# Transposes of the probabilities moved around masks and scores in an attention and expert layer on one core

## The chip, the cores and the metric

The kernel runs on one core of one Trainium2 chip. The metric is the device time in microseconds (us), the median over several executions.

## The reference, cut to what matters

A decoder layer over 32 batches of 128 tokens with 128 features: self-attention with 16 heads of 8 features and a window of 32 keys, then windowed cross-attention over a context (window 16), then a mixture of 8 experts of which each token takes 2. Each part is added to the running x and starts with a layer norm.

```python
x = x + _L0_attn_ref(_layernorm(x), w_qkv, w_out)
x = x + _L0_xattn_ref(_layernorm(x), ctx_1024, Wq, bq, Wk, bk, Wv, bv, Wo, bo, 1)
x = x + _L0_ffn_ref(_layernorm(x), gate_w, w1, w2)
# in both attentions, for each head
attn = einsum('bhqd,bhkd->bhqk', q, k) * scale
attn = softmax(where(allowed, attn, -inf))
out = einsum('bhqk,bhkd->bhqd', attn, v)
```

## The kernel before, in words

Every engine has its own instruction stream, written out by hand, and the streams meet only at semaphores. A batch of 128 tokens is one item. There are 32 items of the self kind and then 32 of the cross kind; one item's tokens lie on the 128 partitions. After both attentions the expert stage runs 71 blocks of 128 sorted rows (lines 985 to 1093).

The attention is a software pipeline. `attend` (line 270) gives every engine one step per item number c. A step works on several items at once: `runs(h, c, lead)` asks whether item c + lead is there, and the code of that lead runs. A loop body (`Fori`) holds four steps. For c from 27 to 32 the last steps of self are interleaved with the first of cross, piece by piece between the `yield`s.

What happens to one item, by lead:

- TensorE, lead 1: masks into p_scores (L401), then the scores added (L408), in two halves of 8 heads. VectorE takes the row maximum of each half (L718) into shift, and TensorE subtracts it with L453. ScalarE takes the exponential of each half out of p_scores into probs (L556).
- TensorE, lead 0: `turn_probs` (L523) transposes the probabilities of one half into p_probsT, four full 128x128 transposes. There is only one bank p_probsT, so the second half can start only when ScalarE has copied the first half out (`copy_probsT`, L550). Then L513 multiplies the transposed probabilities with the values, 32 matmuls of 32 output columns (64 records, as float32 goes in two passes).
- VectorE divides by the sums (L759, L761) and so makes att. In the next step (lead -1) TensorE transposes att (L437), ScalarE copies it (L579), TensorE projects it (L463) and VectorE adds it to x (L677).
- Further ahead, lead 5 or more down to 2: statistics (L739, L747), L661 and L664 on GpSimd, normalisation (L688), transpose xT (L494) and its copy (L597), q and k (L420, L421 for self; L429, L431 for cross), values (L478) and their four copies (L612).
- Self: ScalarE copies q and k out raw (L567), a DMA on SP swaps neighbouring partitions (L339), GpSimd and VectorE rotate (L637, L701, L705). Cross: ScalarE adds the biases (L572, L573). In both kinds GpSimd then spreads k over four head groups (k_heads, L643), which the scores need.
- Cross only, for routing: x after cross-attention is normalised (xn3, L692), transposed (x3T, L487), copied (L601) and multiplied with the gate (L797); VectorE picks two experts and their slots (L864 to L927). ScalarE fills the rows (L834), and GpSimd sends them with two indirect DMAs, L855, right behind k_heads, for tile c - 6.

The order inside a TensorE step before is: masks and scores, q and k, transpose of att, first `turn_probs`, shift, projection, second `turn_probs`, values with x3T and xT, L513. The order inside a ScalarE step before is: raw copy (self) or biases (cross), attT, first copy, first exponential, second copy, second exponential, then xnT, x3T, values, row.

## Time and profile before

| what | value |
|---|---|
| median of 3 runs | 622.54 us |
| lowest, highest | 619.52, 624.52 us |
| time of the profiled execution | 620.3 us |
| its span, first to last instruction | 617.9 us |
| mean granted TensorE clock | 0.925 of 2.4 GHz |
| TensorE matmul busy | 507.6 us (82%) |
| VectorE busy | 386.4 us (63%) |
| ScalarE busy | 335.4 us (54%) |
| GpSimd busy | 311.0 us (50%) |

The shares are means over stages with different limits, so the steps of each stage are to be read by themselves. Self steps run to about 190 us of the span, cross steps to about 430 us, the experts after that. A row of the timeline holds a run of instructions of one line: start, length, engine, line, operation, output and inputs, shape and count, and in brackets how long the engine stood idle before it and for whom. A matmul's start is when it was issued; when its result is there shows at the engine that waits for it.

### The profile page before, as it was taken

How to read it: one execution, taken by the hardware profiler on the slowest of the kernel's cores; microseconds unless marked ns; L12 is line 12 of the kernel's file. 1: busy time of each engine (PE TensorE's matmuls, PEld its weight loads, DVE VectorE, ACT ScalarE, POOL GpSimd, SP SyncE). 2: the span in 40 equal slices, each digit the busy share in tenths (PEclk: the TensorE clock that was granted, in tenths of full speed). 3: DMA queues.
4: the chain of work that ended last, by engine and by line, in shares of the span. 5: the costliest groups of instructions: out<-in, count | busy, mean ns of one | idle time of the engine just before them, and what ended most of it. 6: DMA issues, size and time to landing. Idle time of an engine off the chain costs nothing.

```text
span 617.9 us, 30506 instructions
## 1 busy us (share of the span) xinstructions
PE 507.6 (82%) x11885; PEld 413.1 (67%) x11885; DVE 386.4 (63%) x1314; ACT 335.4 (54%) x981; POOL 311.0 (50%) x417
## 2 busy tenths in 40 slices
PE   1769999999988988879788888886179999999940
PEld 1446777777765665657576666655069999999940
DVE  4537788888864567666666666654526666665626
ACT  1547677777776776666666666653223444333410
POOL 3524445444453446655555555654605555545533
PEclk9979999999999999998989899986559999999985
DMA  7160000000000001100000001000222222222229
GB/s 225 54 275 30 22 27 27 28 25 25 27 22 12 16 13 30 34 29 26 26 26 26 26 27 30 28 30 19 76 49 71 70 66 68 70 65 61 56 94 328
DMA packets 36481, 34.92 MB, mean 57 GB/s; under 512 B 5934, under 2 KB 32688, under 8 KB 36161
## 3 DMA queue, kind: packets, MB, share of 16 engines
q1 hardware_dynamic: 20144, 15.42, 7.9%
q10 hardware_dynamic: 11952, 10.07, 5.8%
q0 software_dynamic: 4320, 8.53, 4.1%
q8 instruction: 45, 0.74, 0.5%
q14 instruction: 20, 0.16, 0.1%
HBM read 18.58 MB, written 11.68 MB: 49 GB/s over the span
## 4 chain that ended last, share of the span: by engine, by line
PE 58%; issue 14%; another core or an unknown queue 13%; DVE 4%; DMA 3%; ACT 3%; SPq 2%; ACTq 1%; POOL 1%; DVEq 0%; POOLq 0%
PE p_scores L1006 9%; PE p_probsT L523 7%; PE p_att_bank L513 6%; PE p_scores L408 5%; PE p_att_bank L1015 5%; PE p_v_bank L1015 5%; PE p_scores L453 3%; PE p_scores L401 2%; PE p_v_bank L478 2%; PE p_att_bank L463 2%; PE p_qk L420 2%; PE p_v_bank L494 2%; DVE x L312 1%; PE p_scores L1021 1%
## 5 line engine op out<-in xcount | busy, mean ns | idle before, releaser
L643 POOL TENSOR_TENSOR k_heads<-qk,consts 128x512 f32<-128x512 f32 x64 | 66.7, 1042 | 121.0 <-ACT qk L573 65.7
L1091 POOL DMA_INDIRECT expert_results<-weighted,result_at x71 | 74.7, 1053 | 77.0 <-DVE weighted L1079 41.4
L718 DVE TENSOR_REDUCE shift<-p_scores 128x8 bf16<-128x512 f32 x128 | 82.4, 686 | 34.1 <-PE p_scores L408 33.9
L550 ACT COPY probsT<-p_probsT 128x512 f32<-128x512 f32 x128 | 75.6, 591 | 26.1 <-PE p_probsT L523 24.5
L513 PE MATMUL p_att_bank<-values,probsT 128*32 128x36 f32 x4096 | 66.6, 205 | 24.9 <-issue 24.9
L1055 ACT ACTIVATE hidden<-p_scores 128x512 f32<-128x512 f32 x71 | 42.4, 598 | 77.2 <-PE p_scores L1006 52.2
L523 PE MATMUL p_probsT<-consts,probs 128*128 128x128 f32 x512 | 83.1, 287 | 0.5 <-ACT probsT L550 0.2
L513 PEld LDWEIGHTS p_att_bank<-values,probsT 128*32 128x32 f32 x4096 | 53.3, 111 | 39.6 <-issue 32.9
L556 ACT ACTIVATE probs<-p_scores 128x512 f32<-128x512 f32 x128 | 77.9, 609 | 0.1
L1006 PE MATMUL p_scores<-gotT,w_now 128*128 128x128 f32 x568 | 77.8, 281 | 0.0
L855 POOL DMA_INDIRECT sent_rows<-row,slot_u x64 | 64.3, 1004 | 15.8 <-issue 15.5
L1006 PEld LDWEIGHTS p_scores<-gotT,w_now 128*128 128x128 f32 x568 | 71.5, 198 | 0.2 <-ACT gotT L1058 0.2
L612 ACT COPY values<-p_v_bank 32x128 f32<-32x128 f32 x256 | 68.3, 267 | 2.2
L408 PE MATMUL p_scores<-k_heads,qk 32*32 32x256 f32 x2048 | 64.9, 405 | 3.5 <-issue 3.5
L523 PEld LDWEIGHTS p_probsT<-consts,probs 128*128 128x128 f32 x512 | 61.8, 148 | 6.5 <-ACT probsT L550 6.3
L677 DVE TENSOR_TENSOR x<-x,p_att_bank 128x128 f32 (+1 forms) x64 | 18.4, 287 | 55.3 <-PE p_att_bank L463 55.3
L1070 DVE COPY w_now<-w 128x512 f32 x71 | 30.5, 430 | 35.8 <-PE p_scores L1006 29.2
L664 POOL TENSOR_TENSOR rstd<-var_eps,minus_half 128x2 f32<-128x2 f32 (+1 forms) x70 | 44.8, 639 | 5.5
L688 DVE TENSOR_SCALAR xn<-x,mean_var,rstd 128x128 f32 (+1 forms) x64 | 42.2, 659 | 6.2 <-POOL rstd L664 6.2
L453 PE MATMUL p_scores<-shift,minus_ident_bf 128*128 128x256 bf16 x256 | 41.8, 283 | 0.6 <-DVE shift L718 0.4
L597 ACT COPY xnT<-p_v_bank 128x128 f32<-128x128 f32 x64 | 17.3, 270 | 44.9 <-remote 37.0
L1015 PE MATMUL p_att_bank<-w_now,hidden 128*128 128x128 f32 x288 | 39.6, 282 | 1.2 <-ACT hidden L1055 1.1
(131 smaller groups left out, 962.6 us busy)
## 6 DMA issues: line engine op xcount, KB each, us to landing
got<-sent_rows ACTq DMA_DIRECT2D x71, 66.0 KB, 1.9
swapped<-raw SPq DMA_DIRECT2D x64, 64.0 KB, 1.9
w<-w_in ACTq DMA_DIRECT2D x2, 2048.0 KB, 11.9
back<-expert_results SPq DMA_DIRECT2D x8, 512.0 KB, 6.8
ctxT<-ctxT_in SPq DMA_DIRECT2D x32, 64.0 KB, 1.9
out<-x SPq DMA_DIRECT2D x8, 256.0 KB, 5.0
x<-x_in SPq DMA_DIRECT2D x4, 448.0 KB, 10.1
expert_results<-weighted,result_at POOLq DMA_INDIRECT x71
```

Source lines behind the costliest of these rows:

```text
L408: mm = nc.tensor.matmul(p_scores[j * BLK:(j + 1) * BLK, r * G:(r + 1) * G, 0:WIN], qk[r * BLK:(r + 1) * BLK, 0, j * BLK:(j + 1) * BLK], k_ ...
L513: mm = nc.tensor.matmul(p_att[j * BLK:(j + 1) * BLK, r * VROW:(r + 1) * VROW], probsT[:, 4 * (r // HALF) + 2 * ks + r % HALF, j * BLK:(j + ...
L523: mm = nc.tensor.transpose(p_probsT[:, i * P:(i + 1) * P], probs[:, half, ks, r * G:(r + 1) * G, :].rearrange("p g k -> p (g k)"), ident)
L550: nc.scalar.copy(probsT[:, 4 * half:4 * half + 4, :], p_probsT[:, :].rearrange("p (m q) -> p m q", q=P)).then_inc(s_pT, 1)
L556: nc.scalar.activation(probs[:, half, :, :, :].rearrange("p s h k -> p h s k"), p_scores[:, half * 8:half * 8 + 8, 0:WIN].rearrange("p h ( ...
L612: a = nc.scalar.copy(values[lo:lo + BLK, slot, 1:, :, g, 0:HD], p_v[lo:lo + BLK, :].rearrange("p (b r d) -> p b r d", b=NBLK, d=HD))
L643: nc.gpsimd.tensor_tensor(k_heads[:, :, BLK:], qk[:, 1:2, :].to_broadcast([P, G, P]), cv(C_HEAD, G).unsqueeze(2).to_broadcast([P, G, P]), ...
L718: nc.vector.tensor_reduce(shift[:, half * 8:half * 8 + 8], p_scores[:, half * 8:half * 8 + 8, 0:WIN], AX.X, ALU.max).then_inc(s_max, 1)
L855: nc.gpsimd.indirect_dma_start(out=sent, out_offset=bass.IndirectOffsetOnAxis(ap=slot_u[:, t, k:k + 1], axis=0), in_=row[:, t, k, :], in_o ...
L1006: mm = nc.tensor.matmul(p_hidden[half][:, f * P:(f + 1) * P], w1_now[:, half, f * P:(f + 1) * P], gotT[:, half, :], start=True, stop=True)
L1015: mm = nc.tensor.matmul(p_y[half], hidden[:, half, f * P:(f + 1) * P], w2_now[:, half, f * P:(f + 1) * P], start=(f == 0), stop=(f == FC - 1))
L1091: nc.gpsimd.indirect_dma_start(out=results, out_offset=bass.IndirectOffsetOnAxis(ap=result_at[:, slot:slot + 1], axis=0), in_=weighted[:, ...
```

## The change

The first `turn_probs` of an item moves to the front of the TensorE step, ahead of masks and scores; it now waits for the first exponential of its item, which the masks' wait covered before. The second moves right behind the scores. On ScalarE both copies of p_probsT stand first in the step and both exponentials one behind the other; the raw copy of the self kind moves behind the exponentials, and in the cross kind the bias passes stand behind the second copy. GpSimd, VectorE and SP have the same order as before.

```diff
@@ pe_step @@
+                if runs(h, c, 0):
+
+                    n = count(0)
+                    nc.tensor.wait_ge(s_probs, 2 * n + 1)
+                    wait(nc.tensor, s_pT, 2 * n)
+                    turn_probs(0).then_inc(s_pTraw, 1)
+                yield
                 if runs(h, c, 1):
...
                         mm.then_inc(s_scores, 1)
                 yield
+                if runs(h, c, 0):
+
+                    n = count(0)
+                    if not runs(h, c, 1):
+                        nc.tensor.wait_ge(s_probs, 2 * n + 2)
+                    nc.tensor.wait_ge(s_pT, 2 * n + 1)
+                    turn_probs(1).then_inc(s_pTraw, 1)
+                yield
                 if own and runs(h, c, 3):
...
-                if runs(h, c, 0):
-
-                    n = count(0)
-                    if not runs(h, c, 1):
-                        nc.tensor.wait_ge(s_probs, 2 * n + 2)
-                    wait(nc.tensor, s_pT, 2 * n)
-                    turn_probs(0).then_inc(s_pTraw, 1)
-                yield
                 if runs(h, c, 1):
...
-                yield
-                if runs(h, c, 0):
-
-                    n = count(0)
-                    nc.tensor.wait_ge(s_pT, 2 * n + 1)
-                    turn_probs(1).then_inc(s_pTraw, 1)
                 yield
@@ act_step @@
+                if runs(h, c, 0):
+                    copy_probsT(0)
+                yield
+                if runs(h, c, 0):
+                    copy_probsT(1)
+                yield
+                if not own and runs(h, c, 2):
+
+                    n = count(2)
+                    nc.scalar.wait_ge(s_qkraw, n + 1)
+                    nc.scalar.activation(qk[:, 1, :], p_qk[:, P:2 * P], ACT.Identity, bias=cols[:, 1:2])
+                    nc.scalar.activation(qk[:, 0, :], p_qk[:, 0:P], ACT.Identity, bias=cols[:, 0:1]).then_inc(s_qk, 1)
+                yield
+                if runs(h, c, -1):
...
+                yield
+                if runs(h, c, 1):
+                    exponent(0)
+                yield
+                if runs(h, c, 1):
+                    exponent(1)
+                yield
                 if own and runs(h, c, 3):
...
                     nc.scalar.copy(raw[:, (c + 3) % 2, :, :].rearrange("p t k -> p (t k)"), p_qk[:, 0:2 * P]).then_inc(s_raw, 1)
-                if not own and runs(h, c, 2):
...
-                yield
-                if runs(h, c, -1):
...
-                yield
-                if runs(h, c, 0):
-
-                    copy_probsT(0)
-                yield
-                if runs(h, c, 1):
-                    exponent(0)
-                yield
-                if runs(h, c, 0):
-                    copy_probsT(1)
-                yield
-                if runs(h, c, 1):
-                    exponent(1)
-                yield
                 if runs(h, c, 3 + ahead):
```

The changed kernel has a few lines more, so its line numbers run on: masks L408, scores L415, q and k L435, L436 (self) and L444, L446 (cross), att's transpose L452, shift L460, projection L470, values L479, L514 for the probabilities times values, L524 for their transposes, and on ScalarE copies L551, exponentials L557.

TensorE at the start of the first step of the cross loop, before (p_probsT is the bank of the transposed probabilities, p_qk holds q and k):

```order
L401 MATMUL p_scores<-masks_bf,ident_bf 32x4x64 x15
L408 MATMUL p_scores<-k_heads,qk 32x4x64 x16
L425 REGISTER_ALU
L429 MATMUL p_qk<-xnT,wcross 128x128 [waits xT_made]
L430 ISA
L431 MATMUL p_qk<-ctxT,wcross 128x128 [waits ctx_loaded0]
L436 REGISTER_ALU
L437 MATMUL p_att_bank<-consts,att 128x128 [waits att_made]
L294 REGISTER_ALU
L523 MATMUL p_probsT<-consts,probs 128x128 [waits probsT_made]
L523 MATMUL p_probsT<-consts,probs 128x128 x3
```

The same place in the changed kernel:

```order
L524 MATMUL p_probsT<-consts,probs 128x128 [waits probsT_made,probs_made]
L524 MATMUL p_probsT<-consts,probs 128x128 x3
L294 ISA
L404 REGISTER_ALU [waits probs_made]
L408 MATMUL p_scores<-masks_bf,ident_bf 32x4x64 [waits qk_spread]
L408 MATMUL p_scores<-masks_bf,ident_bf 32x4x64 x15
L415 MATMUL p_scores<-k_heads,qk 32x4x64 x16
L524 MATMUL p_probsT<-consts,probs 128x128 [waits probsT_made]
L524 MATMUL p_probsT<-consts,probs 128x128 x3
L440 REGISTER_ALU
L444 MATMUL p_qk<-xnT,wcross 128x128 [waits xT_made]
```

One set of four transposes now stands ahead of the masks and one between the scores and q, k.

ScalarE at the same place, before:

```order
L572 ACTIVATE qk<-p_qk,cols 128x128 [waits qk_in_psum]
L573 ACTIVATE qk<-p_qk,cols 128x128
L578 REGISTER_ALU
L579 COPY attT<-p_att_bank 128x128 [waits attT_in_psum]
L549 ISA
L550 COPY probsT<-p_probsT 128x512 [waits probsT_in_psum]
L555 ISA
L556 ACTIVATE probs<-p_scores 128x8x2x32 [waits scores_shifted]
```

And in the changed kernel:

```order
L551 COPY probsT<-p_probsT 128x512 [waits probsT_in_psum]
L550 REGISTER_ALU
L551 COPY probsT<-p_probsT 128x512 [waits probsT_in_psum]
L572 REGISTER_ALU
L573 ACTIVATE qk<-p_qk,cols 128x128 [waits qk_in_psum]
L574 ACTIVATE qk<-p_qk,cols 128x128
L580 COPY attT<-p_att_bank 128x128 [waits attT_in_psum]
L556 ISA
L557 ACTIVATE probs<-p_scores 128x8x2x32 [waits scores_shifted]
```

Both copies now stand ahead of the bias passes and the exponentials.

## Rows read from the trace of the kernel before

**Rows 1.** Busy time in a stretch: engines PE, PEld, DVE, ACT, POOL; then clock, DMA share, GB/s.

```profile
238.97:411.76 172.79, 144.29 (x3901) 109.11 (x3903) 109.42 (x464) 111.86 (x346) 101.60 (x139) 0.94 0.09 28
```

**Rows 2.** Timeline of TensorE in a self step.

```profile
155.32 0.27 PE L437 MATMUL p_att_bank<-consts,att 128*128 128x128 f32 x1
155.43 0.60 PE L523 MATMUL p_probsT<-consts,probs 128*128 128x128 f32 x4
155.87 0.60 PE L453 MATMUL p_scores<-shift,minus_ident_bf 128*128 128x256 bf16 x4
156.31 0.38 PE L463 MATMUL p_att_bank<-wself,attT 128*128 128x128 f32 x2
156.71 0.66 PE L523 MATMUL p_probsT<-consts,probs 128*128 128x128 f32 x4
157.29 0.46 PE L478 MATMUL p_v_bank<-wself,xnT 128*32 128x32 f32 x32
157.68 0.33 PE L494 MATMUL p_v_bank<-consts,xn 128*128 128x128 f32 x1
157.94 0.77 PE L513 MATMUL p_att_bank<-values,probsT 128*32 128x36 f32 x64
```

**Rows 3.** Timeline of TensorE in a cross step.

```profile
353.67 0.33 PE L401 MATMUL p_scores<-masks_bf,ident_bf 32*32 32x256 bf16 x16
...
354.63 0.49 PE L429 MATMUL p_qk<-xnT,wcross 128*128 128x128 f32 x2
...
357.29 0.46 PE L478 MATMUL p_v_bank<-wcross,ctxT 128*32 128x32 f32 x32
...
358.38 0.49 PE L513 MATMUL p_att_bank<-values,probsT 128*32 128x36 f32 x12
...
360.15 0.77 PE L513 MATMUL p_att_bank<-values,probsT 128*32 128x36 f32 x50 [0.51 <-issue]
360.87 0.33 PE L401 MATMUL p_scores<-masks_bf,ident_bf 32*32 32x256 bf16 x16
```

**Rows 4.** Timeline of ScalarE in the same cross step.

```profile
354.73 0.40 ACT L834 COPY row<-xn 128x256 f32<-128x256 f32 x1
...
355.65 0.36 ACT L573 ACTIVATE qk<-p_qk,cols 128x128 f32<-128x128 f32 x1
...
360.48 0.27 ACT L597 COPY xnT<-p_v_bank 128x128 f32<-128x128 f32 x1 [1.99 <-remote]
```

**Rows 5.** Timeline of GpSimd in the same cross step.

```profile
356.17 1.04 POOL L643 TENSOR_TENSOR k_heads<-qk,consts 128x512 f32<-128x512 f32 x1 [1.55 <-ACT qk L573]
357.38 1.06 POOL L855 DMA_INDIRECT sent_rows<-row,slot_u  x1 [0.17 <-issue]
358.74 0.96 POOL L855 DMA_INDIRECT sent_rows<-row,slot_u  x1 [0.30 <-issue]
```

**Rows 6.** Timeline of TensorE, GpSimd and VectorE around 412 us, late in the cross stage.

```profile
412.39 2.53 PE L408 MATMUL p_scores<-k_heads,qk 32*32 32x256 f32 x32
...
413.87 0.95 POOL L855 DMA_INDIRECT sent_rows<-row,slot_u  x1 [0.31 <-issue]
...
415.38 1.29 DVE L718 TENSOR_REDUCE shift<-p_scores 128x8 bf16<-128x512 f32 x2 [2.42 <-PE p_scores L408]
```

**Rows 7.** Timeline of TensorE, GpSimd and ScalarE around 423 us.

```profile
423.47 1.06 PE L523 MATMUL p_probsT<-consts,probs 128*128 128x128 f32 x4
...
423.44 0.96 POOL L855 DMA_INDIRECT sent_rows<-row,slot_u  x1 [0.30 <-issue]
...
424.56 0.59 ACT L550 COPY probsT<-p_probsT 128x512 f32<-128x512 f32 x1 [1.26 <-issue]
```

**Rows 8.** ScalarE in a self step, and from the page's DMA issues the swap.

```profile
153.67 1.10 ACT L612 COPY values<-p_v_bank 32x128 f32<-32x128 f32 x4
155.52 0.37 ACT L567 COPY raw<-p_qk 128x256 f32<-128x256 f32 x1 [0.74 <-PE p_qk L421]
...
swapped<-raw SPq DMA_DIRECT2D x64, 64.0 KB, 1.9
```

9 lines of the change are left out of this document (4 added, 5 removed).

## The prediction, made before the changed kernel was run

> **What bounds the kernel now.** I read the busy table by stretch first, then the engines' timelines inside one step of each stage. The run has two attention stages of 32 steps and then the expert stage, which holds no line of the change. The stretch of 172.79 us in the row is the part of the cross stage in which GpSimd sends routed rows: 23 periods from one such step to the next, so 7.51 us each, with TensorE counted busy for 144.29 of it at a granted clock of 0.94 [rows 1]. A self step takes 4.84 us and TensorE is hardly ever idle in it, so there its own order and its waits decide.
>
> In the self step the reader should compare starts. The first four transposes go from 155.43 to 155.87, 0.44 us. The two matmuls of the projection start at 156.31, which at 0.11 us each should end the issue at 156.53, but the second transposes start at 156.71: 0.18 us of waiting for ScalarE's copy out of the single bank p_probsT. They then take 0.58 up to L478, and of the 0.14 above 0.44 some part is the change from full-array matmuls to 32-wide tiles: L494 to L513 is 0.26, where one full matmul to the next (L437 to L523) is 0.11 [rows 2].
>
> In the cross step the period is 353.67 to 360.87, 7.20 us, and TensorE is not the limit. From 358.38 its L513 matmuls stop after 12 and the last 50 start at 360.15 [rows 3]. ScalarE waits 1.99 us for results of matmuls that had been issued at 357.29 and just after [rows 3, 4]. GpSimd has k_heads at 356.17 and then its two indirect sends, 357.38 to 358.44 and 358.74 to 359.70 [rows 5]. I read this as TensorE frozen while GpSimd prepares the sends: the L478 tiles issued at 357.29 give their results only some 0.6 us after the second send. Two other places say which matmuls freeze. L408, again 32-wide tiles, is stretched to 2.53 us over the sends that end at 414.82, and VectorE waits 2.42 us for it [rows 6]. Full 128x128 transposes issued at 423.47, inside a send of 423.44 to 424.40, are done on time: ScalarE copies their output at 424.56 [rows 7].
>
> So the cross step is a ring, and its parts add up to the period. End of second send to next mask L401: 360.87 - 359.70 = 1.17. Mask and scores to qk: 354.63 - 353.67 = 0.96 [rows 3, 5]. qk matmuls to the end of the second ScalarE pass: 355.65 + 0.36 - 354.63 = 1.38 [rows 3, 4]. Gap 0.16, k_heads 1.04, gap 0.17, two sends 2.32 [rows 5]. Sum 7.20.
>
> **The change in the cross stage.** It adds no instruction and removes none; VectorE and GpSimd keep their order. TensorE now has the first transposes between L513 and the masks, and the second between the scores and qk. Both places are inside the ring; before, both sets stood after qk, beside ScalarE, k_heads and the sends, where they cost nothing. First transposes 0.44, second 0.44, and one more change from full array to tiles, 0.15 at most: 0.88 to 1.03 a step, I take 0.95. ScalarE's second copy now stands ahead of its qk passes. It can start some 0.17 after the second transposes and holds ScalarE about 0.5 us, while the qk matmuls and their latency take 0.75, so it just fits and costs nothing; without that cover it would be up to 0.5.
>
> Whether the ring stays closed depends on L513. The path to it (attT copy, projection, residual add, normalisation, x3T) hangs on qk as the sends do. Before, L513 started 1.00 us after the first send, and needs 0.72 (360.15 to 360.87) [rows 3, 5]. The second transposes no longer stand in that path, but the normalisation is what ended last in it, so L513 still starts about 1 us into 2.32 us of sends. If its tiles freeze like those of L478 and L408, the ring goes through it: release, 0.72 of L513, then the new pieces. This is unknown for L513 by itself, as it was never first in the queue when a send began.
>
> The step is slower by 0.95 when warm. The mean clock of 0.94 means that some 12 in 100 of the time is at half speed, where the added matmuls cost twice: 1.05. From the code the sends share a step with k_heads and L513 in 24 steps (c = 6 to 29): 24 x 1.05 = 25 us.
>
> There is a second term. L478 moves ahead by the second transposes, 0.5 us or so, and would then finish within 0.2 us of the first send, on one side or the other. Where it is late, it freezes, and ScalarE's copies (xnT, x3T, four values, row) come after the release as before, ending at 354.73 + 0.40 = 355.13, 1.46 after the mask's start of before, thus after the end of L513 [rows 3, 4]. The first copy is now queued behind them and the second transposes behind that copy: 1.46 + 0.59 + 0.05 = 2.10, where TensorE would be ready at 0.44 + 0.96 = 1.40 to 1.55. That is 0.55 to 0.70 a step (somewhat more in every second step, where ScalarE also makes ratios). From none to all steps it is 0 to 17 us; I take a quarter of the steps, 4 us.
>
> **The change in the self stage.** Removed: the wait of 0.18 and part of the 0.14 behind it, as masks and scores (0.96) now stand between the transposes and cover the copy of 0.59 [rows 7]. Added: one more change to tiles, up to 0.15. Left: between -0.2 and +0.05 for TensorE. ScalarE then becomes an equal: the first copy is queued behind the four values copies, 1.10 us from 153.67, and the raw copy (0.37) moves behind both exponentials [rows 8]. My sum around ScalarE's ring (copy, second transposes, copy, attT, two exponentials, raw, xnT, values) is near 4.75. The raw copy, which followed qk at once, now ends about 1.9 us later in the step, as the shift matmuls and two exponentials at 0.5 us each come first. Its DMA takes 1.9 us [rows 8], and the rotation needs it in the next step; that uses up nearly all of the slack, so the bound on the other side is +0.2. I take -0.08 over some 28 full steps: -2 us, range -5 to +6. Cross steps without sends (some 8) may gain or lose 0.2 each; nothing.
>
> **Sum.** The profiled execution took 620.3 us, its span 617.9. 620.3 + 25 + 4 - 2 = 647. The median of the runs shown is 622.54, 2.2 above; I forecast 649.
>
> **A rule weighed against this.** The rows show tiles held through both sends, gaps included [rows 3 to 6]. The Trainium skill ("TensorE: Matmul & The Clock Gate", Part 2, step-by-step) gives TensorE two SBUF read ports of its own, and "DMA: Bandwidth & Descriptors" (SWDGE vs HWDGE vs iDMA) tells only of VectorE holding up GpSimd's writing of descriptors. By these nothing holds L513, which is the first rival's case; the trace disagrees for L478 and L408 and is silent on L513.
>
> **Rivals.**
> - L513 runs through the sends. For: full-array matmuls do, and L513 was never seen alone. Against: it has the 32-wide weights of L478. Then TensorE is free again before the sends end. From the start of qk, L513 begins at 358.38 - 354.63 = 3.75, then 0.72 for it, 0.44 + 0.15 for the first transposes, 0.96 for mask and scores, 0.44 for the second: 6.5 a step, 0.7 less than 7.2, over 24 steps -17. With -2 from the self stage: 603, about 605 by the median. It decides for faster from the point where L513 is not held at all.
> - All L478 freeze as well, and the clock stays low longer since TensorE stands still more: 25 + 17 + 5 for the clock = 667.
> - The order does little: L513 is held for only part of the sends (released with the first one), which gives back 1.3 of the 2.32 and pays 1.05: within 1 us a step of now; 615 to 630.
>
> **How the numbers follow.** Forecast 0.70, first rival 0.16, second 0.07, third 0.07. The forecast's own range is 638 (0.88 a step, no late L478, -5) to 664 (1.05, most L478 late, +3). To leave out no more than 2 in 10 with both ends, the range takes in the first rival: 603 to 664. What a measurement here can tell from no change is about 1%, 616 to 629. Slower by more than that: forecast, second rival and a little of the third, 0.78. Within: 0.05. Faster: 0.17.
>
> **What would show it.** Right: cross steps of 8.0 to 8.9 us between masks; L513 stopping within a send, with xnT and x3T copied by ScalarE during the sends and not after; 0.44 us of transposes between L513 and mask and between scores and qk; first exponential right before the second. The self step stays at 4.7 to 4.85, with no 0.18 gap ahead of the second transposes. Wrong: L513 all issued within 0.8 us while a send runs, and cross steps near 6.5 (first rival); a self step over 4.95, where ScalarE's order or the swap would be the limit.

## The result, and the profile after

The changed kernel took 680.9 us, the median of 4 runs (674.73 to 682.33). The kernel before, run beside it, took 621.03 us (4 runs, 614.23 to 624.52). The ratio is 1.0985, with a 95% interval of 1.086 to 1.111. The forecast was 649.0: the direction is right, but the loss is 60 us where 27 was forecast, and the time lies above the range.

The cross stage first, in the busy table by stretch. The row for the same 23 periods between steps that send reads for the changed kernel (columns as in [rows 1]):

```profile
243.50:467.50 224.00, 176.13 (x3896) 126.50 (x3896) 110.52 (x466) 112.01 (x348) 101.57 (x137) 0.78 0.07 22
```

A period is 9.74 us (224.00 / 23), where [rows 1] gave 7.51. The counts of instructions agree to within 5; VectorE, ScalarE and GpSimd are busy for the same time to within 1.1 us. TensorE's busy time grew by 32 us and its mean granted clock fell from 0.94 to 0.78. The clock has two levels here, 1.2 and 2.4 GHz, so some 44% of these 224 us were at the lower one, where it had been 12%.

The same table, one row for each period, from k_heads to k_heads, first for the kernel before:

```profile
318.30:325.54 7.24, 5.88 (x172) 4.58 (x172) 5.06 (x21) 4.65 (x15) 4.43 (x7) 1.00 0.09 28
...
340.55:348.97 8.42, 7.02 (x169) 5.16 (x167) 4.76 (x20) 5.01 (x17) 4.47 (x7) 0.80 0.08 24
```

And for the changed kernel:

```profile
322.37:331.87 9.50, 7.38 (x167) 5.19 (x167) 4.59 (x20) 5.01 (x17) 4.43 (x7) 0.82 0.07 21
...
352.12:360.94 8.82, 6.16 (x172) 4.53 (x172) 5.06 (x21) 4.62 (x15) 4.43 (x6) 1.00 0.07 23
360.94:371.20 10.26, 8.50 (x167) 6.19 (x167) 4.59 (x20) 5.11 (x17) 4.43 (x6) 0.67 0.06 20
```

This is the table to make whenever the clock moves, since it parts the two effects. Over all 23 periods, the 17 of before at clock 1.00 have a mean of 7.27; the 5 of the changed kernel have 8.82. So 1.55 us of the 2.23 are there at full clock, and 0.68 come from more periods with half speed in them. But five are few, and four of them are of the shorter of two kinds that alternate (8.65 to 8.82; the fifth, of the longer kind, took 9.10). In a_filled below, where all 23 periods are at clock 1.00, the mean is 9.00. So at full clock the order costs 1.55 to 1.73 us a period, and the clock adds the other 0.50 to 0.68.

The step from 352.12 is at full clock and can be compared with [rows 3 to 5] piece by piece. TensorE in it:

```profile
352.94 0.46 PE L479 MATMUL p_v_bank<-wcross,ctxT 128*32 128x32 f32 x32
...
354.47 0.37 PE L514 MATMUL p_att_bank<-values,probsT 128*32 128x36 f32 x15
...
356.15 0.77 PE L514 MATMUL p_att_bank<-values,probsT 128*32 128x36 f32 x47 [0.52 <-issue]
...
356.85 0.66 PE L524 MATMUL p_probsT<-consts,probs 128*128 128x128 f32 x4
357.43 0.33 PE L408 MATMUL p_scores<-masks_bf,ident_bf 32*32 32x256 bf16 x16
...
358.98 0.66 PE L524 MATMUL p_probsT<-consts,probs 128*128 128x128 f32 x4 [0.52 <-ACT probsT L551]
359.47 0.39 PE L444 MATMUL p_qk<-xnT,wcross 128*128 128x128 f32 x2
```

ScalarE in the same step:

```profile
356.47 0.27 ACT L597 COPY xnT<-p_v_bank 128x128 f32<-128x128 f32 x1 [3.37 <-remote]
...
357.91 0.41 ACT L834 COPY row<-xn 128x256 f32<-128x256 f32 x1
...
358.34 0.58 ACT L551 COPY probsT<-p_probsT 128x512 f32<-128x512 f32 x1
```

GpSimd:

```profile
352.12 1.04 POOL L643 TENSOR_TENSOR k_heads<-qk,consts 128x512 f32<-128x512 f32 x1 [3.69 <-ACT qk L574]
353.33 1.06 POOL L855 DMA_INDIRECT sent_rows<-row,slot_u  x1 [0.17 <-issue]
354.69 0.96 POOL L855 DMA_INDIRECT sent_rows<-row,slot_u  x1 [0.30 <-issue]
```

The ring is as it was, with the two sets of transposes in it. From the end of the second send (355.65) to the end of L514's issue (356.85) is 1.20, where the forecast's sum has 1.17. Then come 0.58 of transposes to the masks (356.85 to 357.43), and after the scores a wait of 0.52 for the first copy before the second set, which takes 0.49 (358.98 to 359.47). 0.58 + 0.52 + 0.49 = 1.59 against the 1.55 of the table. L514 itself is not stopped entirely: 2 records get through at 355.39, and the last 47 go out from 356.15.

The copy is late by a chain that starts with the sends. L479 was issued at 352.94, 0.39 us ahead of the first send, but ScalarE's xnT copy starts only at 356.47, after the second send and a wait of 3.37. It waits for the full transpose L495 (issued at 354.27), which stands behind L479 in TensorE's queue; since full transposes beside a send are done on time (below), it is L479 that is late. Behind xnT stand x3T, the four values and row, to 358.32, and only then the first copy of p_probsT at 358.34. It is so in all 23 periods of the stretch: xnT starts 0.59 to 0.84 us after the second send ends. The forecast had it in a quarter of them.

What the late copy costs depends on the step. Where ScalarE also makes ratios before it (L842), TensorE's wait at full clock is about 0.89 and not 0.5; a_filled shows the two kinds in turn:

```profile
378.35 0.66 PE L535 MATMUL p_probsT<-consts,probs 128*128 128x128 f32 x4 [0.89 <-ACT probsT L562]
...
387.19 0.66 PE L535 MATMUL p_probsT<-consts,probs 128*128 128x128 f32 x4 [0.51 <-ACT probsT L562]
```

That is 0.70 in the mean. In a step at half clock the masks and scores themselves take so long that the copy is ready in time, and no wait is left:

```profile
366.89 0.44 PE L408 MATMUL p_scores<-masks_bf,ident_bf 32*32 32x256 bf16 x16
...
368.41 1.11 PE L524 MATMUL p_probsT<-consts,probs 128*128 128x128 f32 x4
```

From the masks to the second set are 1.52 us there (clock 0.50), against 1.55 in the step above (357.43 to 358.98, clock 1.00). So the late copy and the low clock partly hide each other, and their prices can't be added from different steps.

The self stage at its steady pace, TensorE in the step that answers to [rows 2]:

```profile
156.66 0.91 PE L415 MATMUL p_scores<-k_heads,qk 32*32 32x256 f32 x32
157.50 0.66 PE L524 MATMUL p_probsT<-consts,probs 128*128 128x128 f32 x4
```

The wait of 0.18 ahead of the second set is gone, as forecast, but the step is not shorter: from item 12 to 28 it mostly takes 4.85 to 4.93, where before it mostly took 4.81 to 4.88, and only every fourth is shorter (5.23, before 5.4 to 5.5). What came in its place was early in the stage, not here. The starts of k_heads (L643), one for each of the 64 items, counted from 0, cut the whole run into stretches. The times are read from the timelines of GpSimd of four executions, among them the two kernels run again on another chip (below):

| from item to item | before | before, again | changed | changed, again |
|---|---|---|---|---|
| 2 to 5 | 21.8 | 22.6 | 26.3 | 25.7 |
| 5 to 30 | 129.2 | 129.3 | 126.7 | 125.6 |
| 30 to 39 | 49.4 | 50.6 | 55.5 | 56.7 |
| 39 to 63 | 179.2 | 179.7 | 230.9 | 229.5 |
| 63 to the end | 210.3 | 206.9 | 211.7 | 211.5 |

In the first pair the differences are +4.5, -2.5, +6.1, +51.7 and +1.4, and make 61.2 of the 61.3 by which the spans differ (679.2 - 617.9). The -2.5 looks like the forecast's -2 but doesn't come from the steady steps: from item 12 to 28 it is 79.37 before and 79.10 changed (79.37 and 79.35 in the second pair). It comes from the steps just behind the late one of the first row (items 5 to 9: 22.3 and 20.5) and from the last, items 29 to 30 (7.24 and 6.09). The first row is a cost that I had not seen at all. GpSimd's part of the rotation and k_heads in this stretch, in the kernel before:

```profile
29.83 0.73 POOL L637 TENSOR_TENSOR turned_sin<-swapped,consts 128x256 f32<-128x256 f32 x1
...
32.59 1.04 POOL L643 TENSOR_TENSOR k_heads<-qk,consts 128x512 f32<-128x512 f32 x1 [2.02 <-DVE qk L705]
```

The changed kernel, ScalarE's raw copy, its queue's load of the expert weights, and GpSimd:

```profile
28.25 0.38 ACT L593 COPY raw<-p_qk 128x256 f32<-128x256 f32 x1
28.31 0.33 ACTq L561 DMA_DIRECT2D w<-w_in  x1
...
40.92 0.72 POOL L637 TENSOR_TENSOR turned_sin<-swapped,consts 128x256 f32<-128x256 f32 x1 [10.94 <-issue]
...
42.27 1.04 POOL L643 TENSOR_TENSOR k_heads<-qk,consts 128x512 f32<-128x512 f32 x1 [0.64 <-DVE qk L705]
```

And the busy table of the changed kernel in the middle of it:

```profile
34.00:40.00 6.00, 0.00 (x0) 0.00 (x0) 0.00 (x0) 0.98 (x5) 0.00 (x0) 0.71 1.02 425
```

ScalarE issues two loads of 2 MB for the experts there, and the DMA engines are fully busy (share 1.02, 425 GB/s) until between 40 and 41 us. The small swap of q and k behind them waits. Before, the raw copy stood first in the step, so one more item had its swap back ahead of the load (turned_sin at 29.83, k_heads at 32.59). With the raw copy behind both exponentials, that item's swap is issued as the loads are, and turned_sin starts only at 40.92. By item 5 about a self step is lost (4.5 us), and part of it is won back behind it: item 9 starts at 72.11 before and at 74.90 changed, 2.8 later (2.3 in the second pair). All traces with the raw copy ahead of the exponentials have item 5 at 48.8 to 51.7, first_set_only among them (49.75), and all with the raw copy behind the exponentials at 53.7 to 55.3. It was read from these traces; no kernel with the load moved was tried.

### The profile page after: what moved, and what is told of

It reads as the page before. It is cut to its first block, busy times and chain, and to the rows that moved or that the text cites. A ratio compares the mean times of both kernels' runs of the same rounds, so it can differ in the third digit from the quotient of the medians.

```text
span 679.2 us, 30539 instructions
## 1 busy us (share of the span) xinstructions
PE 543.2 (80%) x11885; PEld 427.8 (63%) x11885; DVE 385.3 (57%) x1314; ACT 337.4 (50%) x981; POOL 312.2 (46%) x417
## 4 chain that ended last, share of the span: by engine, by line
PE 42%; another core or an unknown queue 29%; issue 13%; DMA 4%; ACT 3%; DVE 3%; SPq 3%; POOL 1%; ACTq 1%; DVEq 0%; POOLq 0%
PE p_scores L1006 9%; PE p_probsT L524 6%; PE p_att_bank L1015 5%; PE p_v_bank L1015 4%; PE p_scores L415 4%; PE p_att_bank L514 4%; PE p_att_bank L470 2%; PE p_v_bank L479 1%; PE p_scores L408 1%; PE p_scores L460 1%; SPq L344 1%; DVE x L312 1%; PE p_scores L1021 1%; PE p_v_bank L495 1%
## 5 line engine op out<-in xcount | busy, mean ns | idle before, releaser
L643 POOL TENSOR_TENSOR k_heads<-qk,consts 128x512 f32<-128x512 f32 x64 | 66.6, 1041 | 163.7 <-ACT qk L574 122.7
L551 ACT COPY probsT<-p_probsT 128x512 f32<-128x512 f32 x128 | 74.9, 585 | 95.4 <-PE p_probsT L524 93.7
L524 PE MATMUL p_probsT<-consts,probs 128*128 128x128 f32 x512 | 101.3, 330 | 8.8 <-ACT probsT L551 6.1
L514 PE MATMUL p_att_bank<-values,probsT 128*32 128x36 f32 x4096 | 70.6, 213 | 35.7 <-issue 25.3
L524 PEld LDWEIGHTS p_probsT<-consts,probs 128*128 128x128 f32 x512 | 65.4, 164 | 47.7 <-ACT probsT L551 38.0
L514 PEld LDWEIGHTS p_att_bank<-values,probsT 128*32 128x32 f32 x4096 | 56.7, 119 | 51.1 <-issue 33.8
L557 ACT ACTIVATE probs<-p_scores 128x512 f32<-128x512 f32 x128 | 70.4, 610 | 4.8 <-PE p_scores L460 4.7
L415 PE MATMUL p_scores<-k_heads,qk 32*32 32x256 f32 x2048 | 70.3, 463 | 1.4 <-issue 1.4
L460 PE MATMUL p_scores<-shift,minus_ident_bf 128*128 128x256 bf16 x256 | 43.3, 291 | 0.0
```

Source lines behind the costliest of these rows:

```text
L415: mm = nc.tensor.matmul(p_scores[j * BLK:(j + 1) * BLK, r * G:(r + 1) * G, 0:WIN], qk[r * BLK:(r + 1) * BLK, 0, j * BLK:(j + 1) * BLK], k_ ...
L514: mm = nc.tensor.matmul(p_att[j * BLK:(j + 1) * BLK, r * VROW:(r + 1) * VROW], probsT[:, 4 * (r // HALF) + 2 * ks + r % HALF, j * BLK:(j + ...
L524: mm = nc.tensor.transpose(p_probsT[:, i * P:(i + 1) * P], probs[:, half, ks, r * G:(r + 1) * G, :].rearrange("p g k -> p (g k)"), ident)
L551: nc.scalar.copy(probsT[:, 4 * half:4 * half + 4, :], p_probsT[:, :].rearrange("p (m q) -> p m q", q=P)).then_inc(s_pT, 1)
L557: nc.scalar.activation(probs[:, half, :, :, :].rearrange("p s h k -> p h s k"), p_scores[:, half * 8:half * 8 + 8, 0:WIN].rearrange("p h ( ...
L643: nc.gpsimd.tensor_tensor(k_heads[:, :, BLK:], qk[:, 1:2, :].to_broadcast([P, G, P]), cv(C_HEAD, G).unsqueeze(2).to_broadcast([P, G, P]), ...
```

## The experiments

The theory from here: the ring through the sends, with L514 held, got longer by the two sets, by the late copy, and by the clock. Its rivals: L514 is not held and something else is late; the loss is in the self order; it is the clock alone. The runs are told by question, not in their order. They fell on several chips, and only ratios against the kernel before on the same chip are compared. The expectations stand as written before each run.

### Which stage carries the loss

The edit puts the change under a condition, with the old order elsewhere: `cross_order_only` has it in the cross steps, `self_order_only` in the self steps (there the condition is `own and c < B + FIRST`). One line of it, the rest follows the same pattern on TensorE and ScalarE. Both kernels were also run unchanged.

```diff
+                new = not own and (not isinstance(h, int) or c >= 1)
-                if runs(h, c, 0):
+                if new and runs(h, c, 0):
                     turn_probs(0)
```

> The kernel before once more, unchanged, for its own trace on the chip of these experiments, where the kernel before took 578 us and not 621. Theory 1 (how long 32-wide tiles are held by a send is a property of the chip; in the first four experiments the longest hold seen was 0.27 us): L478 meets the sends here too but gives its results within about 0.3 us, and the cross step is 6.0 to 6.3 us in place of 7.2-7.5. Rival D (the hold is as long here, and something else is shorter): ScalarE's xnT again 2 us idle, released 0.6 us after the second send, and the time comes from the self or the expert stage.

> The changed kernel, unchanged, on this chip. Theory 1: without the long hold the ring through the sends is open; the change costs what its transposes add to the chain attT, projection, add, x3T, L514, masks, scores: 0.44 + 0.44 + 0.15 and a clock that stays at its high level, 24 to 30 steps, 25-30 us: 603-610 us, a ratio of 1.045-1.055. Rival D: the ratio is 1.09-1.10 as on the first chip, about 632 us.

> The change in the cross steps from the second on alone; self steps and the mixed ones have the old order. Theory 1: nearly all of the cost is here: ratio within 0.01 of that of the changed kernel. Rival E (the self stage and the straight-line steps pay a good part): less than two thirds of the cost.

> The change in the self steps alone, up to the first mixed one. Theory 1: the wait of 0.18 us goes and a change to tiles of 0.15 comes, with ScalarE's ring near 4.8: within 4 us of before. Rival E: 8 us or more slower.

| kernel | median us | ratio to before | 95% |
|---|---|---|---|
| before, again | 618.66 | 0.9997 | 0.9957 to 1.0036 |
| changed, again | 680.25 | 1.0993 | 1.0914 to 1.1072 |
| cross_order_only | 676.02 | 1.0988 | 1.0925 to 1.1051 |
| self_order_only | 622.34 | 1.0081 | 1.0048 to 1.0114 |

(Before beside them: 617.98.) The result repeats on another chip. The first two expectations took the chip for the unusual one of 578 us (below); it was one of the usual kind, so their theory was not tested and rival D's ratio came. Nearly all of the loss is in the cross stage. The self order costs 0.8%, about 5 us, where -2 was forecast, and its cross steps are as before (7.53 us in the mean): its trace has the late item at the weight load (item 5 at 53.7). The two profiled executions differ by only 3.2 us, of which 0.9 are there by item 30; where the rest of the 5 lies isn't shown.

They also part the row from item 30 to 39. Against the 50.6 of before on this chip it is 50.8 in self_order_only, 53.3 in cross_order_only and 56.7 in the changed kernel. So 2.7 of its 6.1 us come with the new order in the cross steps from the second on, and the other 3.4 only with the new order in the mixed steps as well.

### Which of the two moves costs what

`first_set_only` takes the kernel before and moves only the first set of transposes to the front of the step, with the first copy in front on ScalarE. `second_set_behind_qk` takes the changed kernel and puts the second set and its copy behind q and k.

```diff
@@ second_set_behind_qk, pe_step and act_step @@
                         mm.then_inc(s_scores, 1)
...
-                    turn_probs(1).then_inc(s_pTraw, 1)
...
+                    turn_probs(1).then_inc(s_pTraw, 1)
...
-                    copy_probsT(1)
...
                     nc.scalar.activation(qk[:, 0, :], p_qk[:, 0:P], ACT.Identity, bias=cols[:, 0:1]).then_inc(s_qk, 1)
+                    copy_probsT(1)
```

> Only the first transposes move to the front (on ScalarE only the first copy); the second stay behind the projection. On a chip of the 618 kind, theory 1: the ring gets 0.44 + 0.15 us, L478 meets the sends as before, and the first copy is queued behind xnT, x3T, values and row, so ScalarE's q and k passes come 0.2 us later: 0.7 to 0.9 us a step warm, about 640 us, a third to a half of the whole cost. Rival F (ScalarE's queue is what costs, the second transposes nothing): over 665 us.

> The changed kernel with the second transposes (and on ScalarE the second copy) put behind q and k. On a 618 chip, theory 1: 0.44 us leave the ring, and so does the wait for the first copy, as q and k no longer stand behind it: warm steps of 7.7 as with the first set alone, 640-645 us. Rival F (ScalarE's queue is in the way all the same): 655 us or more.

`first_set_only` took 640.81 us against 621.01, ratio 1.0342 (1.0287 to 1.0396). Its 13 periods at clock 1.00 have a mean of 7.82. So the first set costs 0.55 in a warm step: 0.44 of transposes and 0.1 for the change to tiles, the forecast's piece. `second_set_behind_qk` took 662.75 against 623.17, ratio 1.0643 (1.0584 to 1.0703). Its 11 periods at full clock have a mean of 7.86. TensorE in such a step:

```profile
354.17 0.33 PE L408 MATMUL p_scores<-masks_bf,ident_bf 32*32 32x256 bf16 x16
...
355.13 0.49 PE L436 MATMUL p_qk<-xnT,wcross 128*128 128x128 f32 x2
...
355.72 0.66 PE L524 MATMUL p_probsT<-consts,probs 128*128 128x128 f32 x4
```

The q and k matmuls start 0.96 after the masks again (354.17 to 355.13). With the second set between, as in the changed kernel, a warm step is 8.82, so that place costs 0.96: 0.49 for the set and 0.5 for the wait on the copy. Moved behind q and k, both have gone from the ring. So two moves of about the same 0.5 us of matmuls cost 0.55 and 0.96 (these means come mostly from steps without ratios; with ratios the wait is 0.4 longer), and the wait is what makes the second the dearer.

The medians don't say this by themselves. second_set_behind_qk was expected at 640 to 645 and took what its rival F asked for, 655 or more. Its cross steps are as the theory has them; what it loses is in the self stage, which nobody had priced: from item 5 to 30 it takes 136.3 us, where before took 129.2 and the changed kernel 126.7. A steady self step is 5.31 us there, 5.13 in first_set_only and 4.84 before. Each half of the change is slower in the self steps than the whole. The cause isn't shown.

### Is L514 held by the sends, when it stands alone

The first rival of the forecast was that L513 (L514 now) runs through the sends. Here the sends wait until the values' matmuls are done, so that only L514 can meet them.

```diff
                 if not own and (not isinstance(h, int) or c <= B):
+                    if runs(h, c, 2):
+                        nc.gpsimd.wait_ge(s_vraw, count(2) + 1)
                     route_pool(h, c, [c - 6])
```

> The changed kernel with the sends held back until the values matmuls L479 are done, some 0.1-0.3 us later than now. On a chip of the 618 kind, theory 1: L479 is never held, ScalarE copies xnT, x3T and values during the sends, L514 stops alone (some 15 records and then nothing until 0.5 us after the second send), the wait of 0.52 us for the first copy goes: warm steps of 8.3 in place of 8.7, 665-673 us. Rival C (L514 is not held): steps under 7.6, below 640 us. On a chip of the 578 kind nothing is held: 605-615 us.

> The same in the kernel before, where L478 is issued at the time of the first send. On a 618 chip, theory 1: the sends start 0.5 us later, L513 is held in place of L478, ScalarE is free sooner but is not what the ring waits for: steps of 7.6-7.7 in place of 7.2, 628-635 us. Rival C: steps near 6.5 or held scores as with the sends after xT, 600-630 us.

The changed kernel with this took 701.11 us against 623.17, ratio 1.1249 (1.1191 to 1.1306); the kernel before with it 664.71, ratio 1.0654 (1.0587 to 1.0722). TensorE, GpSimd and ScalarE in a step of the first, with the reciprocal on VectorE that reads L514's result:

```profile
343.56 1.06 POOL L857 DMA_INDIRECT sent_rows<-row,slot_u  x1 [1.18 <-PE p_v_bank L479]
343.69 0.67 PE L514 MATMUL p_att_bank<-values,probsT 128*32 128x36 f32 x41
343.87 0.27 ACT L597 COPY xnT<-p_v_bank 128x128 f32<-128x128 f32 x1 [1.55 <-PE p_v_bank L495]
...
344.92 0.96 POOL L857 DMA_INDIRECT sent_rows<-row,slot_u  x1 [0.30 <-issue]
...
346.35 0.45 PE L514 MATMUL p_att_bank<-values,probsT 128*32 128x36 f32 x21 [0.52 <-issue]
346.84 0.26 DVE L761 RECIPROCAL inv_sum<-p_att_bank 128x16 f32<-128x16 f32 x1 [1.26 <-PE p_att_bank L514]
```

The first rival falls. L495, a full matmul of 343.49, is done on time (xnT copied at 343.87, inside the send), and L514 stops after 41, lets out one record at 344.90 and one at 345.63, and goes on at 346.35, after the second send ended at 345.88. The late copy is gone in this kernel, yet it is slower than the changed one: the sends start about 1.0 us later after k_heads (2.22 here, 1.21 in the changed kernel), and since L514 is held by itself, the ring goes through that delay in full. Both expectations were too low (665 to 673 and 628 to 635): I had counted on the copy and forgotten the ring. In the kernel before the values stand behind the projection and the second transposes, so the sends there start 2.6 to 4.4 us after k_heads and not 0.5 later.

### What is held, and what happens when the sends are moved

`sends_after_scores` puts the two sends ahead of k_heads, where q and k, the transposes and the projection run; `sends_after_xT` lets them wait for L494's result. Each was made from the kernel before (b_) and from the changed one (a_). The first four fell on a chip on which the kernel before takes 578.26 us, so two were run again, with one of the changed ones, on a chip of the usual kind (621.01).

```diff
@@ sends_after_scores @@
+                if not own and (not isinstance(h, int) or c <= B):
+                    if runs(h, c, 2):
+                        wait(nc.gpsimd, s_scores, 2 * count(2))
+                    route_pool(h, c, [c - 6])
                 if runs(h, c, 2):
...
-                if not own and (not isinstance(h, int) or c <= B):
-                    route_pool(h, c, [c - 6])
@@ sends_after_xT @@
                 if not own and (not isinstance(h, int) or c <= B):
+                    if runs(h, c, 3):
+                        nc.gpsimd.wait_ge(s_xTraw, count(3) + 1)
                     route_pool(h, c, [c - 6])
```

> The kernel before, with the two sends of routed rows moved from behind k_heads to the front of GpSimd's cross step, where they start as soon as the scores are done. Theory 1 (32-wide tiles are held while GpSimd prepares sends, full-array matmuls are not): the sends lie beside q and k, transposes, shift and projection, which take 354.63 to 357.29 in a step of before, so nothing is held but perhaps the first L478 tiles. The cross step falls from 7.2 to 5.4-5.9 us and the kernel to 580-592 us, though k_heads comes up to 0.9 us later. Rival A (any matmul that meets a send is held): q and k are held until 0.6 us after the sends, ScalarE's passes and k_heads wait for them, the cross step grows to 8.5 us or more and the kernel to 650 us. Rival B (the sends hold nothing, the cross step is bound by VectorE's and ScalarE's chains): within 1 us a step of before, 600-640 us, with k_heads late.

> The changed kernel with the same move of the sends. Theory 1: nothing is held, the loss of the change shrinks to what its transposes cost in the chain through L514, the normalisation and x3T: from q and k at 359.47 to L514 at 363.16 is 3.7, then 0.7 for it, 0.6 for the first transposes, 0.96 for mask and scores, 0.5 for the second: 6.4 us a step in place of 9.7, about 600-610 us in all. Still 15 to 25 us over the kernel before with the same move. Rival A: q and k held, steps of 9.5 us or more, 680 us or over. Rival B: about 680 us as it is.

> The kernel before, with the sends held back until the transpose xT of the same step is done, so that L513 alone stands before TensorE when they start. Theory 1 with L513 of the same kind as L478: ScalarE copies xnT and x3T during the sends, L513 stops after some 15 records and resumes 0.5 us after the second send; steps grow by 1.2 us (the sends start at 358.6 in place of 357.4), 24 of them, to about 650 us. Rival C (L513 is not of the kind that is held, only L478 and L408 are): L513 is done within 0.8 us of xT, the scores behind it are held in its place and resume as soon as the sends end, steps near 6.3 us, about 600 us.

> The changed kernel with the sends held back until xT is done. L479 is then never held, so ScalarE's xnT, x3T and values copies run during the sends, and the first copy of p_probsT is no longer queued behind them. Theory 1: the 0.52 us that TensorE waits for that copy (0.5 to 1.0 a step) goes, and 1.2 us of later sends comes: steps of 9.2 warm in place of 8.8, 685-700 us. In the profile no wait of L524 on the first copy. Rival C: L514 runs at once and the steps fall to about 7, 610-620 us.

> As b_sends_after_xT, again, since the chips differ: on one the kernel before takes 578 us and 32-wide tiles were held 0.05 to 0.27 us by a send, on another 618 us with holds of 2.4 us. On a chip of the 618 kind, theory 1 (L513 is held like L478): xnT is copied during the sends, L513 stops within them and resumes 0.5 us after the second, steps of 8.4 us, 640-650 us. Rival C (L513 is never held): L513 done within 0.8 us, then masks or scores held in its place, 595-605 us. On a chip of the 578 kind: 584 us again.

> The changed kernel with the sends held back until xT is done. On a chip of the 618 kind, theory 1: L514 alone is held, the wait for the first copy behind ScalarE's copies is gone (0.5 to 1.0 us a step), the sends start 1.2 us later: 685-700 us. Rival C: 620-640 us. On a chip of the 578 kind: 611 us again.

> The kernel before with the sends at the front of GpSimd's step. On the 578 chip this cost 27 us, not by TensorE but by VectorE: its xn3 took 1.75 us in place of 0.35 while GpSimd worked. On a chip of the 618 kind, theory 1 (only 32-wide tiles are held, full-array matmuls are not): the same step of 7.4 us as there, since no tile meets a send for long, 604-615 us, faster than before for once. Rival A (full-array matmuls are held there too): q and k held behind the sends, 8.5 us or more a step, 650 us.

| kernel | before beside it | median us | ratio | 95% | mean period |
|---|---|---|---|---|---|
| b_sends_after_scores | 578.26 | 605.63 | 1.0491 | 1.0439 to 1.0542 | 7.37 |
| a_sends_after_scores | 578.26 | 631.72 | 1.0904 | 1.0852 to 1.0955 | 8.03 |
| b_sends_after_xT | 578.26 | 583.61 | 1.0113 | 1.0047 to 1.0179 | 6.52 |
| a_sends_after_xT | 578.26 | 611.29 | 1.0564 | 1.0517 to 1.0610 | 7.16 |
| b_sends_after_xT_2 | 621.01 | 629.27 | 1.0135 | 1.0082 to 1.0187 | 8.08 |
| a_sends_after_xT_2 | 621.01 | 667.44 | 1.0767 | 1.0716 to 1.0818 | 9.17 |
| b_sends_after_scores_2 | 621.01 | 614.58 | 0.9883 | 0.9832 to 0.9935 | 7.40 |

Few of these expectations came true. On the first chip they took the hold for granted: 580 to 592 and 600 to 610 were put for the sends after the scores, and 605.63 and 631.72 came. On the usual chip b_sends_after_xT_2 took 629.27, between its theory and its rival, and so did a_sends_after_xT_2 with 667.44. Neither says anything on L513: it is issued about 1 us ahead of the first send (at 335.38 and 345.74, the sends at 336.44 and 346.72), and it is the scores that meet the sends.

The same kernel, b_sends_after_xT, on the two chips shows what differs. In both the scores meet the sends. On the chip of 578 us:

```profile
335.90 1.02 PE L408 MATMUL p_scores<-k_heads,qk 32*32 32x256 f32 x32
...
336.06 1.06 POOL L857 DMA_INDIRECT sent_rows<-row,slot_u  x1 [1.75 <-PE p_v_bank L494]
...
336.85 0.49 PE L429 MATMUL p_qk<-xnT,wcross 128*128 128x128 f32 x2
```

On the chip of 621 us:

```profile
336.21 1.19 PE L408 MATMUL p_scores<-k_heads,qk 32*32 32x256 f32 x30
...
336.44 1.06 POOL L857 DMA_INDIRECT sent_rows<-row,slot_u  x1 [2.50 <-PE p_v_bank L494]
...
337.77 0.37 PE L408 MATMUL p_scores<-k_heads,qk 32*32 32x256 f32 x1 [0.37 <-issue]
337.80 0.96 POOL L857 DMA_INDIRECT sent_rows<-row,slot_u  x1 [0.30 <-issue]
...
338.80 0.49 PE L429 MATMUL p_qk<-xnT,wcross 128*128 128x128 f32 x2
```

From the start of the scores to q and k is 0.95 on the first and 2.59 on the second. The sends themselves take the same time. So the hold is there on the five usual chips and all but absent on the chip of 578 us. The four kernels ran on that one on a single occasion, so chip and occasion can't be told apart. There the change still costs 4.5 points in this version (1.0564 to 1.0113), 0.64 us a period, with hardly any time at 1.2 GHz (3 us of its 23 periods): this pair is the slower with the change without hold and without clock. On the usual chip it costs 6.3 points (1.0767 to 1.0135) and 1.09 a period. What the plain changed kernel takes on that chip was not tried.

Full matmuls are not held. In a step of b_sends_after_scores_2 at clock 1.00 the projection (L463) and the second transposes lie beside the sends:

```profile
364.46 1.06 POOL L857 DMA_INDIRECT sent_rows<-row,slot_u  x1 [0.25 <-issue]
...
365.27 0.47 PE L463 MATMUL p_att_bank<-wcross,attT 128*128 128x128 f32 x2
365.58 0.60 PE L523 MATMUL p_probsT<-consts,probs 128*128 128x128 f32 x4
365.83 0.96 POOL L857 DMA_INDIRECT sent_rows<-row,slot_u  x1 [0.30 <-issue]
365.97 0.29 DVE L679 TENSOR_TENSOR x<-x,p_att_bank 128x128 f32 x1 [1.25 <-PE p_att_bank L463]
...
366.18 1.78 DVE L690 TENSOR_SCALAR xn<-x,mean_var,rstd 128x128 f32 x1
366.21 0.59 ACT L550 COPY probsT<-p_probsT 128x512 f32<-128x512 f32 x1 [0.73 <-PE p_probsT L523]
```

The projection of 365.27 is read at 365.97 and the transposes of 365.58 are copied at 366.21, 0.70 and 0.63 us after their issue; in the step of [rows 3 to 5], with no send beside them, it was 0.70 (356.46 to 357.16) and 0.64 (356.76 to 357.40). (The clock matters when such rows are compared: the transposes of [rows 7] and the end of the scores of [rows 6] are at clock 0.50, where the scores of 367.08 in the changed kernel take 1.40 us with no send beside them. So of the 2.53 us of [rows 6] only some 1.1 is hold, by estimate.)

What is not shown is whether the width of the tile is what counts. Every group that was held is also one of many small matmuls, 32 or 64 records in 0.5 to 0.9 us, and every group that passed has at most four. No run puts a few 32-wide tiles, or many full ones, beside a send.

b_sends_after_scores_2 beats the kernel before on this usual chip, by 1.2%, and no more. k_heads now starts as the second send ends (366.81 after 366.79), and the normalisation of 366.18 takes 1.78 us; which of the two sets the period of 7.40 (7.37 on the other chip) no run parts. On the chip without the hold this version is a loss of 4.9%.

### How much of it is the clock

In `a_filled` the changed kernel gets 8 matmuls a cross step whose result nobody reads: 3 behind the shift and 5 between the values and x3T. `b_filled` puts 6 into the kernel before, `b_sends_and_fill` 8 into b_sends_after_scores.

```diff
@@ a_filled, the five @@
+                    if runs(h, c, 0):
+                      nc.tensor.wait_ge(s_pT, 2 * count(0) + 2)
+                      for _ in range(5):
+                        nc.tensor.matmul(p_probsT[:, 0:2 * P].rearrange("p (g k) -> p g k", g=G), ident_bf[:, :], ones_bf[:, 0:WIN].unsqueeze(1).to_broadcast([P, G, WIN]),
+                                         start=True, stop=True, skip_group_check=True)
                     nc.tensor.wait_ge(s_xn3, n + 1)
                     nc.tensor.transpose(p_x3T, xn3[:, (c - 2) % 4, :], ident).then_inc(s_x3Traw, 1)
```

> The changed kernel with eight matmuls of 256 bfloat16 columns more in each cross step, three ahead of the wait for attT and five ahead of the wait for xn3, where TensorE is idle for 0.36 and 0.7 us; their results, written into the free bank of the transposes, are not used. Theory 1 (about 0.65 us a step of the change is the clock, at 1.2 GHz for 97 of the 224 us, since TensorE stands still more): the time at 1.2 GHz falls under 60 us and the kernel gets 8-15 us faster, 666-673 us. Rival G (the clock does not go by such gaps): time at 1.2 GHz as before, 680-690 us.

> The kernel before with six matmuls of 256 bfloat16 columns ahead of the wait for xn3 in each cross step, results not used. If the clock costs by the time at 1.2 GHz, the 17-20 us of it in the cross stage go to 0 and 4-7 us come off (612-618 us on a 618 chip), since every step is then one of 7.1-7.3 us. Rival G (the gain in the changed kernel came from something else in the order): no change or 3-4 us slower.

> The kernel before with the sends at the front of GpSimd's step and eight such matmuls ahead of the wait for xn3, where TensorE was idle for 1.7 us. With the sends alone it took 614.6 where before took 621.0, with 27 us at 1.2 GHz in the cross stage. If that goes too: 600-608 us on a 618 chip. On a chip of the 578 kind 595-602 us, slower than before there. Rival G: 614 us or more.

`a_filled` took 663.46 us against 623.17, ratio 1.0658 (1.0600 to 1.0717), where the changed kernel has 1.0985 and 1.0993. All its periods are at full clock, as this one:

```profile
344.16:353.05 8.89, 7.22 (x181) 5.25 (x180) 5.06 (x21) 4.64 (x15) 4.44 (x6) 1.00 0.07 23
```

In the changed kernel some 97 of the 224 us were at 1.2 GHz, here none, and the mean period went from 9.74 to 9.00 (about 8.9 and 9.2 in turn, the longer where ScalarE also makes ratios ahead of the first copy). So 3 points of the 10, about 20 us, go with the low clock; 6.6 points stay at full clock. Part of these 20 us is not the change's doing, since the kernel before has low clock too (7.51 a period, 7.27 at clock 1.00). What the change added by the clock is (9.74 - 9.00) - (7.51 - 7.27) = 0.50 a period, about 12 us over the 23.

`b_filled` took 623.37 against 614.82, ratio 1.0129 (1.0090 to 1.0169), so more clock was no gain for the kernel before, against the expectation (612 to 618). Its profiled execution has all 23 periods at clock 1.00 and a mean of 7.37 (169.48 / 23), but that one took 615.96 us and was the lowest of its five; the others took 622.42 to 624.64. Where those lose 7 us the trace doesn't show. `b_sends_and_fill` took 608.80, ratio 0.9899 (0.9868 to 0.9931), the same as the sends moved alone (0.9883), though all its periods are at clock 1.00 too.

## Why the prediction was wrong in size, by its own steps

- **The ring.** Right. The parts of the sum of 7.20 are all found again, and the change put both sets into it. In a warm step (one at full clock) they measure 0.55 (first_set_only) and 0.49, 1.04 together, where 0.88 to 1.03 was forecast. That is 25 us over 24 steps at full clock; the forecast's 25 had 2.4 us of low clock in it.
- **L513 held.** Right, and shown for L513 alone by the two kernels whose sends wait for the values. The first rival (603) and the third (held in part) fall.
- **"From none to all steps it is 0 to 17 us; I take a quarter of the steps, 4 us."** This step failed, and by the parts that a_filled shows it is the larger miss. L479 has all 32 tiles to get through before the first send, and though it is issued 0.31 to 0.52 us ahead of it in 22 of the 23 periods (in one just behind it), its results were late in all 23. The price of one was right, 0.51 and 0.89 in turn at full clock, 0.70 in the mean, where 0.55 to 0.70 and somewhat more in every second step was put: 16 us over 23 periods in place of 4. The working put L478's end "within 0.2 us of the first send, on one side or the other", which is a toss between 0 and 17, and 4 was not read from any row.
- **The clock.** This step failed too. The forecast kept the mean clock of 0.94 and only let the added matmuls cost twice in its cold share, 2.4 us; the second rival gave 5 us more. Longer waits in every step took the clock of the stretch to 0.78: 0.50 us a period by a_filled, 12 us. (By the five full-clock periods of the changed kernel it would be 0.68, 16 us, and the late copy 12; the two hide each other in part, and only their sum, 28, is firm.) The granted clock of the kernel before was already 0.77 to 0.81 in 6 of the 23 periods, so it stood near the edge, and that was to be read from the trace.
- **The self stage.** The wait of 0.18 went as forecast, but -0.08 a step did not come: 16 steady steps changed by -0.3 and 0.0 us. That the stretch from item 5 to 30 shows -2.5 and -3.7 is luck. Not forecast at all was the step lost at the load of the expert weights, +4.5 us by item 5 and 2.8 by item 9. The prediction saw that the raw copy's swap had used up its slack, and priced that at the swap's median of 1.9 us; it did not ask where in the run that transfer takes ten.
- **"Cross steps without sends (some 8) may gain or lose 0.2 each; nothing."** Items 30 to 39 cost 6.1 us, 2.7 of them by the order in the cross steps and 3.4 only with the mixed steps in the new order too. In the changed kernel item 31 starts 7.12 us after item 30, where before took 4.37, and the two steps from 181.20 to 193.10 have a clock of 0.86. What delays them stays open.

The sum with measured terms: 24 + 16 + 12 for the 23 periods of the cross steps, -2.5 + 4.5 for the self stage, 6 for the hand-over and 1.4 behind it make 61. The profiled executions differ by 60.8 (681.1 - 620.3). The second rival (667) was the nearest case; its 17 us for the late copy was right, and its clock, 5 us and the 2.4 inside the 25, was too small by 5 us or more.

## What to carry to other kernels

Look for the ring through what cannot be moved, here the sends, and price every piece that a new order puts into it, the queues behind a late result among them; where a term hangs on a race of 0.2 us, forecast both ends and not a fraction. If waits get longer while the granted clock is already below 1.00 in some steps, make the table of periods with their clocks and charge the clock for more of them. A wait priced at full clock and a clock priced in other steps may overlap, so check them against a kernel in which one of the two is gone. A total that comes out as forecast is no sign that its parts did: look at the steady steps by themselves. And ask of every moved transfer what else uses the queue and the DMA engines at its worst moment, not at its median.

## What the runs showed of the hardware that was not expected

- While GpSimd's indirect sends run, groups of many matmuls in tiles of 32 (L408, L415, L479, L514) are held on the usual chips, but for one or two records every 0.75 us or so, and small groups of full-width ones are let through: 0.96 us of scores took 2.59. On one chip of those used the hold is nearly absent, and the kernel before takes 578 us there and 615 to 623 on the others. An order tuned for the hold (b_sends_after_scores: 0.988 and 1.049) can be a gain on one and a loss on the other.
- Eight discarded matmuls a step kept the granted clock at 1.00 through a stage that had it at 0.78, and made the changed kernel 3% faster; in the kernel before, with 0.94, six of them gained nothing (1.3% slower by the median, while the profiled execution was 0.2% slower).
- A normalisation on VectorE that takes 0.34 us elsewhere took 1.75 in b_sends_after_scores, on the chip of 578 us, while a send ended and k_heads ran, and TensorE waited for it. It ended 0.09 us after k_heads (342.38 and 342.29); on the usual chip the one of 366.18 above did the same (367.96 and 367.86).

```profile
340.25 0.96 POOL L857 DMA_INDIRECT sent_rows<-row,slot_u  x1 [0.30 <-issue]
...
340.63 1.75 DVE L694 TENSOR_SCALAR xn<-x,mean_var,rstd 128x128 f32 x1
...
342.43 0.33 PE L487 MATMUL p_v_bank<-consts,xn 128*128 128x128 f32 x1 [1.72 <-DVE xn L694]
```
